# Query projections of a graph attention pass: three chunks made first, the others beside the first nine edge groups

## The chip, the cores and the metric

The kernel runs on one core of a Trainium2 chip. The metric is the device time of one execution in microseconds (us); lower is better. Engines: TensorE (PE, its weight loads PEld), VectorE (DVE), ScalarE (ACT), GpSimd (POOL), and SyncE (SP), which issues transfers. Engines run their own instruction streams and wait for each other through semaphores.

## The reference

A graph attention layer over 6250 nodes and 200,000 edges (sorted by destination), and then a mixture of eight experts over the nodes. What matters here is the attention:

```python
enh = node_features + 0.1 * query_emb            # node_features = layernorm(x), 6250 x 256
Q, K, V = enh @ Wq + bq, enh @ Wk + bk, enh @ Wv + bv      # 4 heads of 64
mod_k = K[src] + 0.2 * rel_w[edge_type][:, None, :]
scores = einsum('ehd,ehd->eh', Q[dst], mod_k) / 8          # softmax over the edges of a dst
agg = segment_sum(softmax_weight * V[src], dst)
x = x + layernorm(agg @ Wo + bo + node_features)
```

## The kernel before

The program has three stages, one after the other: `prepare`, `edge_pass` and `finish`, with a barrier of all engines (L645) between the first two. (`any_order_pass` stands under a condition on `unfit` and runs only for edges of an unusual order.)

**prepare.** 49 tiles of 128 nodes: layer norm, transposes into `QT` (features down the partitions, 2 x 6250 columns), K and V projections on TensorE, rows of K and V stored to DRAM (`kv`, 2 KB a node). Beside it VectorE works through a generator `setup()`, a step at a time between its tile operations: it makes each edge group's first node (`bases`), tests whether the edges are in the order that the pass needs (`unfit`), and casts the lists of source nodes, turned by TensorE into `psR`, into `idxall` (L914).

**edge_pass.** First `QT` is projected in place to the queries: 13 chunks `QCH` of 512 columns (the last 106). TensorE multiplies a chunk by `wq` into psD or psK in turn (L446, signal `s_q`), ScalarE adds the bias and copies it back over `QT` (L266, signal `s_qe`); TensorE may be two chunks ahead. Ahead of that, ScalarE copies the source lists of the first six groups from `idxall` into `idx` (`listed`, L256, signal `s_idx`), for which GpSimd's gathers wait.

Then 261 groups. A group is 384 edges of each of two streams (the lower and the upper half of the edges). Its 768 rows of K and V are gathered by six indirect DMAs of 128 rows that GpSimd issues (L246) into a ring of U = 6 slots; the gathers of group g + 6 wait for the sum of group g (`s_agg`). The engines are interleaved by `step(T)`: in the step of group g, TensorE turns the keys of g + 1 (`k_turned`, psK, L461), makes the scores of g (psD, L477 to L485), sums group g - 1 (psA, L496), hands on carried maxima and relation terms (psX, L525 and L527) and turns the weights of g (psP, L534). VectorE's `k_half` (L368) and ScalarE's (L291) copy the turned keys out; VectorE takes the maximum of psD (L393), ScalarE the exponentials (L311), the carried sums (`e_carried`, L302, which waits for the sum of a group) and the turned weights (L323). ScalarE also copies the 16-node windows of `QT` that group g + 1 needs, at offsets `bases`, into `qb` (L285). Steps from -1 to 7 are written out (`LO`, `WARM`), the rest is a loop of six steps a turn, with a short tail.

Groups 0 to 8 read only the start of each stream's range of nodes.

## Time and profile before

| | |
|---|---|
| median of 3 runs | 3803.58 us (3799.91 to 3803.76) |
| profiled execution, its own time | 3804.72 us |
| its span (first to last instruction) | 3802.4 us |
| TensorE busy | 3098.0 us, 81% |
| VectorE, ScalarE, GpSimd busy | 1690.1, 1507.6, 1962.7 us |
| mean granted TensorE clock | 0.870 of full |

Times in the rows are us from the start of the span. "Idle before <- X" tells how long the engine stood still ahead of an instruction and whose signal ended it; "remote" is a signal whose sender the profile doesn't name, "issue" is time with no wait that it shows. A matmul's start is recorded and its end is modelled.

### The profile page before, as it was taken

What the parts mean: (1) busy time and instruction counts of PE and PEld (TensorE: products, weight loads), DVE (VectorE), ACT (ScalarE), POOL (GpSimd) and SP (SyncE); (2) the same over time, 40 slices, a digit from 0 to 9 for tenths busy, and PEclk for the clock granted to TensorE, in tenths of its full rate; (3) what the DMA queues carried; (4) which work ended last, traced back from release to release, by engine and by line L of the source; (5) the groups of instructions that cost most, each with busy time, mean ns of one, the idle gap of its engine ahead of it and who ended that gap; (6) DMA issues with size and microseconds to landing.
All of it is one profiled execution on the core that took longest, in us unless ns stands there. A gap on an engine that the chain in (4) does not pass through costs nothing. (4 is left out here: it accounts for less than half of the span.)

```text
span 3802.4 us, 76627 instructions
## 1 busy us (share of the span) xinstructions
PE 3098.0 (81%) x21156; PEld 2146.9 (56%) x21156; DVE 1690.1 (44%) x6041; ACT 1507.6 (40%) x4739; POOL 1962.7 (52%) x2036
## 2 busy tenths in 40 slices
PE   8777787778777777877777777787667998899898
PEld 6444444444444444444444444444347898888798
DVE  6154444444444444444444444444475554553222
ACT  5333333333333333333333333333336565564232
POOL 6345555555555555655555555555345444432222
PEclk9888888888888888888888888888758999999999
DMA  6556766676666666666667666666475666665664
GB/s 221 164 150 187 191 190 184 186 191 189 185 185 191 189 185 188 187 192 185 189 187 190 188 185 187 190 188 185 138 230 151 203 203 184 194 180 156 194 181 131
DMA packets 292073, 700.68 MB, mean 184 GB/s; under 512 B 44040, under 2 KB 139679, under 8 KB 291796
## 3 DMA queue, kind: packets, MB, share of 16 engines
q0 software_dynamic: 151888, 455.79, 43.4%
q1 hardware_dynamic: 140036, 243.15, 21.0%
q8 instruction: 64, 1.05, 0.1%
q14 instruction: 85, 0.70, 0.1%
HBM read 632.80 MB, written 65.96 MB: 184 GB/s over the span
## 5 line engine op out<-in xcount | busy, mean ns | idle before, releaser
L246 POOL DMA_INDIRECT e_kv<-d_kv,e_idx x1566 | 1496.1, 955 | 1132.3 <-PE psA L496 668.5
L496 PE MATMUL psA<-e_kv,e_probT 128*32 128x128 f32 x6264 | 529.2, 286 | 297.9 <-issue 292.3
L393 DVE TENSOR_REDUCE e_small<-psD 128x1 f32<-128x384 f32 x261 | 145.5, 558 | 1219.6 <-remote 1208.6
L461 PE MATMUL psK<-consts,e_kv 128*128 128x128 f32 x3132 | 606.6, 327 | 3.3 <-ACT QT L266 1.0
L302 ACT ACTIVATE e_carried<-psA,e_small 128x130 f32<-128x130 f32 x261 | 96.7, 370 | 1135.1 <-PE psA L496 1115.4
L496 PEld LDWEIGHTS psA<-e_kv,e_probT 128*32 128x32 f32 x6264 | 199.9, 108 | 532.8 <-issue 503.8
L461 PEld LDWEIGHTS psK<-consts,e_kv 128*128 128x128 f32 x3132 | 427.5, 166 | 116.4 <-issue 110.0
L1975 PE MATMUL f_psY<-f_w,f_hT 128*128 x1680 | 396.6, 390 | 38.2 <-ACT f_hT L1570 22.1
L1500 POOL DMA_INDIRECT out<-f_y,f_whose x105 | 166.8, 1589 | 479.0 <-DMA out<-f_y,f_whose 281.7
L1962 PE MATMUL f_psH<-f_xT,f_w 128*128 128x128 f32 x3360 | 404.3, 280 | 0.4 <-issue 0.4
L1570 ACT ACTIVATE f_hT<-f_psH,f_b 128x128 f32<-128x128 f32 x840 | 237.6, 372 | 411.0 <-PE f_psH L1962 333.1
L1962 PEld LDWEIGHTS f_psH<-f_xT,f_w 128*128 128x128 f32 x3360 | 396.6, 196 | 3.0 <-issue 0.8
L1975 PEld LDWEIGHTS f_psY<-f_w,f_hT 128*128 128x128 f32 x1680 | 317.7, 195 | 86.2 <-issue 45.8
L285 ACT COPY e_qb<-QT 64x32 f32 x1044 | 229.3, 220 | 298.6 <-issue 279.5
L368 DVE COPY e_kT<-psK 128x384 f32<-128x384 f32 x522 | 286.7, 549 | 94.3 <-PE psK L461 84.0
L485 PE MATMUL psD<-e_kT,e_qb 128*32 128x384 f32 x2088 | 293.5, 644 | 0.0
L291 ACT COPY e_kT<-psK 128x384 f32<-128x384 f32 x522 | 247.0, 473 | 30.6 <-issue 23.9
L525 PE MATMUL psX<-e_small,e_carry 128*128 128x1 f32 x522 | 107.8, 271 | 174.2 <-DVE e_small L399 150.7
L525 PEld LDWEIGHTS psX<-e_small,e_carry 128*128 128x128 f32 x522 | 87.1, 207 | 246.4 <-issue 244.0
L534 PE MATMUL psP<-consts,e_prob 128*128 128x128 f32 x783 | 180.8, 352 | 49.5 <-ACT e_prob L311 42.0
L507 PEld LDWEIGHTS psA<-e_accs,e_carry 128*128 128x128 f32 x522 | 90.3, 218 | 227.2 <-issue 227.2
L1821 DVE TENSOR_SCALAR f_xT<-f_psT,f_ln 128x128 f32<-128x128 f32 x210 | 76.5, 406 | 307.8 <-PE f_psT L1952 218.9
(281 smaller groups left out, 4330.2 us busy)
## 6 DMA issues: line engine op xcount, KB each, us to landing
f_w<-in_W SPq DMA_DIRECT2D x113, 1024.0 KB
e_rows<-d_feat SPq DMA_DIRECT2D x174, 288.0 KB
e_kv<-d_kv,e_idx POOLq DMA_INDIRECT x1566
d_accs<-e_accs SPq DMA_DIRECT2D x87, 195.0 KB
f_xs<-d_xs SPq DMA_DIRECT2D x105, 129.0 KB
d_kv<-p_kv SPq DMA_DIRECT2D x48, 256.0 KB, 2.1
p_x<-in_x SPq DMA_DIRECT2D x49, 128.0 KB, 2.6
n_v<-d_kv SPq DMA_DIRECT2D x49, 128.0 KB
```

What stands on the lines that cost most here:

```text
L246: pool.indirect_dma_start(out=kv[g.slot][:, t, :], out_offset=None, in_=kv_dram[:, :], in_offset=bass.IndirectOffsetOnAxis(ap=idx[g.slot][ ...
L285: act.copy(qb[a.slot % R][o * HD:(o + 1) * HD, :].rearrange("p (c b w o) -> p c b w o", c=2, b=DC, o=2)[:, c, :, :, o], QT[o * HD:(o + 1) ...
L291: act.copy(kT[a.slot % 2][:, 1, j * GH:(j + 1) * GH], psK[:, 1, 0:GH]).then_inc(s_kTa, 1)
L368: dve.tensor_copy(kT[a.slot % 2][:, 0, j * GH:(j + 1) * GH], psK[:, 0, 0:GH]).then_inc(s_kTv, 1)
L461: mm = pe.transpose(psK[:, half, t * P:(t + 1) * P], kv[a.slot][:, third * TS + t, half * P:(half + 1) * P], ident)
L485: mm = pe.matmul(psD[own, g.slot % 2, 0:GH], qb[g.slot % R][:, own], kT[g.slot % 2][:, b, c * GH:(c + 1) * GH], start=False, stop=True, ti ...
L496: mm = pe.matmul(psA[own, 0:2 * HD], probT[c.slot % R][:, j, own], kv[c.slot][:, s * TS + j, D + b * P:D + (b + 1) * P], start=j == 0, sto ...
L525: pe.matmul(psX[:, 0:1], carry[a.slot][:, :], small[(a.slot - 1) % U][:, MM], start=True, stop=True)
L534: mm = pe.transpose(psP[:, j * P:(j + 1) * P], prob[g.slot % R][:, j * P:(j + 1) * P], ident)
L1570: act.activation(hT[:, f, :], psH[:, f // FB % 2, f % FB * BK:(f % FB + 1) * BK], ACT.Gelu, bias=b1[:, bass.ds(e * FC + f, 1)]).then_inc(s ...
L1962: mm = pe.matmul(psH[:, f // FB % 2, f % FB * BK:(f % FB + 1) * BK], w1[g % RW][:, a, f * P:(f + 1) * P], xT[g % 2][:, a, :], start=a == 0 ...
L1975: mm = pe.matmul(psY[:, 0:D], hT[:, f, :], w2[:, bass.ds(e * (FC * D) + f * D, D)], start=f == 0, stop=f == FC - 1)
```

## The change

Three query chunks, `EARLY = (0, 5, 6)`, are made ahead of the groups; the two streams' first nine groups read within them. The other ten are cut into 19 units of up to 256 columns (`LATER`), given to the steps -1 to 7 as 1, 3, 3, 2, 2, 2, 2, 2, 2 (`beside`). A unit is `ask(u)` on TensorE, into a PSUM bank of its own, `psL`, and `asked(u)` on ScalarE, which adds the bias and copies it over `QT`. From the second unit on, TensorE waits for the copy of the unit before. The first unit of a step with several stands behind the scores on TensorE and behind the exponentials on ScalarE; the others stand at the step's end. ScalarE waits at the end of such a step until its own copies are written, and ahead of the step's units until its window copies are.

The test `unfit` gets three more conditions, in `setup()`: that group 8's windows end within the chunks made first, and that the second stream doesn't begin ahead of chunk 5. If one fails, the fallback pass runs.

The six first row lists are copied by VectorE in `prepare`, at the end of `setup()`, and the buffers `idx` are allocated outside of both stages. GpSimd waits for `s_idx` from group 6 on only.

```diff
--- before.py
+++ after.py
@@ -137,7 +137,15 @@
 CONSTS, CAT = lay_constants()
 
 
-def edge_pass(nc, ctx, cst, QT, kv_dram, idxall, feat_dram, accs_dram, bases, delta, penc, relT, reach, keys, spots, wq, bqc):
+RING = 6
+EARLY = (0, 5, 6)
+QC = 512
+QH = QC // 2
+SURE = 8
+LATER = [(q, min(q + QH, N)) for c in range(-(-N // QC)) if c not in EARLY for q in range(c * QC, min(c * QC + QC, N), QH)]
+
+
+def edge_pass(nc, ctx, cst, idx, QT, kv_dram, idxall, feat_dram, accs_dram, bases, delta, penc, relT, reach, keys, spots, wq, bqc):
 
 
     def sb(name, shape, dt=F32):
@@ -146,9 +154,8 @@
     def sem(name):
         return ctx.enter_context(nc.semaphore(name))
 
-    U = 6
+    U = RING
     R = 3
-    idx = [sb(f"e_idx{i}", [P, TG], I32) for i in range(U)]
     rows = [sb(f"e_rows{i}", [P, HB, 2, GH], BF16) for i in range(U // HB)]
     kv = [sb(f"e_kv{i}", [P, TG, 2 * D]) for i in range(U)]
     relhot = [sb(f"e_relhot{i}", [P, GH], F32R) for i in range(R)]
@@ -172,6 +179,7 @@
     psP = ctx.enter_context(nc.psum_tensor("psP", [P, 512], F32))
     psA = ctx.enter_context(nc.psum_tensor("psA", [P, 512], F32))
     psX = ctx.enter_context(nc.psum_tensor("psX", [P, 512], F32))
+    psL = ctx.enter_context(nc.psum_tensor("psL", [P, DC, QH], F32))
     MX, MC, MM, NM, AL, SUM = (slice(i, i + 1) for i in range(6))
     CARRIED = slice(256, 256 + 2 * CW)
 
@@ -201,10 +209,13 @@
     s_px = sem("es_px")
     s_q = sem("es_q")
     s_qe = sem("es_qe")
-    QCH = [slice(q, min(q + 512, N)) for q in range(0, N, 512)]
+    QCH = [slice(c * QC, min(c * QC + QC, N)) for c in EARLY]
     psQ = (psD, psK)
 
     LO, HI, WARM = -1, 2, 8
+    share = [1, 3, 3] + [2] * (WARM - LO - 3)
+    beside = {LO + i: list(range(sum(share[:i]), sum(share[:i + 1]))) for i in range(WARM - LO)}
+    assert WARM <= SURE and sum(share) == len(LATER)
     AHEAD = U - 1
     SOON = NT - (NG + LO - WARM) // U
     assert 0 <= SOON < WARM
@@ -241,7 +252,7 @@
 
                     if g.first >= U:
                         pool.wait_ge(s_agg, g.t - (U - 1))
-                    hold(pool, s_idx, g.t + 1)
+                        hold(pool, s_idx, g.t - (U - 1))
                     for t in range(TG):
                         pool.indirect_dma_start(
                             out=kv[g.slot][:, t, :], out_offset=None, in_=kv_dram[:, :],
@@ -257,9 +268,6 @@
                          idxall[:, 0:2 * NG * TS].rearrange("p (c q) -> p c q", c=2)[:, :, bass.ds(t * TS, TS)]
                          ).then_inc(s_idx, 1)
 
-            for t in range(U):
-                listed(t, t)
-
             for i, q in enumerate(QCH):
                 act.wait_ge(s_q, i + 1)
                 for b in range(DC):
@@ -267,6 +275,13 @@
                                    bias=bqc[:, b:b + 1]).then_inc(s_qe, 1)
             act.wait_ge(s_qe, DC * len(QCH))
             act.wait_ge(s_init, 4)
+
+            def asked(u):
+                lo, hi = LATER[u]
+                act.wait_ge(s_q, len(QCH) + u + 1)
+                for b in range(DC):
+                    act.activation(QT[:, b, lo:hi], psL[:, b, 0:hi - lo], ACT.Identity, bias=bqc[:, b:b + 1]
+                                   ).then_inc(s_qe, 1)
 
             def step(T):
                 n = T(-AHEAD)
@@ -313,6 +328,11 @@
                                    accum_out=small[g.slot][:, SUM]).then_inc(s_exp, 1)
                     act.activation(small[g.slot][:, AL], small[g.slot][:, MC], ACT.Exp,
                                    bias=small[g.slot][:, NM], scale=SCALE).then_inc(s_exp, 1)
+                units = beside.get(g.t, []) if isinstance(g.t, int) else []
+                if units and a.live:
+                    act.wait_ge(s_qb, a.t * 4 + 4)
+                for u in units[0:-1][0:1]:
+                    asked(u)
                 if a.live:
                     k_half(a, 1)
                 if g.live:
@@ -321,6 +341,10 @@
                         act.wait_ge(s_agg, g.t - (R - 1))
                     act.wait_ge(s_pp, g.t + 1)
                     act.copy(probT[g.slot % R][:, :, :].rearrange("p t q -> p (t q)"), psP[:, 0:GH]).then_inc(s_pT, 1)
+                for u in units[len(units[0:-1][0:1]):]:
+                    asked(u)
+                if units:
+                    act.wait_ge(s_qe, DC * (len(QCH) + units[-1] + 1))
             pipeline(act, NG, -AHEAD, HI, U, WARM, step)
 
         @blk.vector
@@ -449,8 +473,19 @@
             pe.wait_ge(s_qe, DC * len(QCH))
             pe.wait_ge(s_init, 4)
 
+            def ask(u):
+                lo, hi = LATER[u]
+                if u >= 1:
+                    pe.wait_ge(s_qe, DC * (len(QCH) + u))
+                for b in range(DC):
+                    for a in range(DC):
+                        mm = pe.matmul(psL[:, b, 0:hi - lo], wq[:, a, b * P:(b + 1) * P], QT[:, a, lo:hi],
+                                       start=a == 0, stop=a == DC - 1)
+                mm.then_inc(s_q, 1)
+
             def step(T):
                 g, a = T(0), T(-1)
+                units = beside.get(g.t, []) if isinstance(g.t, int) else []
 
                 def k_turned(j):
 
@@ -486,6 +521,8 @@
                                            kT[g.slot % 2][:, b, c * GH:(c + 1) * GH],
                                            start=False, stop=True, tile_position=(0, own.start))
                     mm.then_inc(s_d, 1)
+                for u in units[0:-1][0:1]:
+                    ask(u)
                 c = T(1)
 
                 def summed(j):
@@ -533,6 +570,8 @@
                     for j in range(TS):
                         mm = pe.transpose(psP[:, j * P:(j + 1) * P], prob[g.slot % R][:, j * P:(j + 1) * P], ident)
                     mm.then_inc(s_pp, 1)
+                for u in units[len(units[0:-1][0:1]):]:
+                    ask(u)
             pipeline(pe, NG, LO, HI, U, WARM, step)
 
 
@@ -550,7 +589,7 @@
     return [(lo, bass.ds(node_rows(t) + lo, hi - lo), hi) for lo, hi in zip(cuts, cuts[1:])]
 
 
-def prepare(nc, ctx, cst, io, out, dram, QT, idxall, bases, delta, penc, relT, unfit, reach, keys, wq, wo, bqc, consts,
+def prepare(nc, ctx, cst, io, out, dram, idx, QT, idxall, bases, delta, penc, relT, unfit, reach, keys, wq, wo, bqc, consts,
             lnst, biaso):
 
 
@@ -593,6 +632,7 @@
     endsf = sb("p_endsf", [P, IT, P])
     misfit = sb("p_misfit", [P, 2 * len(chunks) + 2])
     misfits = sb("p_misfits", [P, 2])
+    early = sb("p_early", [1, 4])
     psT = [ctx.enter_context(nc.psum_tensor(f"p_psT{i}", [P, 512], F32)) for i in range(2)]
     psKV = [[ctx.enter_context(nc.psum_tensor(f"p_ps{n}{i}", [P, 512], F32)) for i in range(2)] for n in "KV"]
     psS = ctx.enter_context(nc.psum_tensor("p_psS", [P, 512], F32))
@@ -899,7 +939,15 @@
                     link(dve.tensor_copy(baseall[a * HW:(a + 1) * HW, :],
                                          reach[a * HW:(a + 1) * HW, a * NG:(a + 1) * NG]))
                 yield
-                link(dve.tensor_scalar(unfit[0:1, :], misfits[0:1, 1:2], 1.0, None, ALU.min))
+                link(dve.tensor_scalar(early[:, 0:1], basef[0:1, 0, SURE:SURE + 1], float(QC - W), None, ALU.is_gt))
+                link(dve.tensor_scalar(early[:, 1:2], basef[0:1, 1, 0:1], float(EARLY[1] * QC), None, ALU.is_lt))
+                yield
+                link(dve.tensor_scalar(early[:, 2:3], basef[0:1, 1, SURE:SURE + 1],
+                                       float((EARLY[2] + 1) * QC - W), None, ALU.is_gt))
+                link(dve.tensor_copy(early[:, 3:4], misfits[0:1, 1:2]))
+                yield
+                link(dve.tensor_reduce(misfits[0:1, 0:1], early[:, :], AX.X, ALU.add))
+                link(dve.tensor_scalar(unfit[0:1, :], misfits[0:1, 0:1], 1.0, None, ALU.min))
                 yield
                 link(dve.memset(delta[:, 0:1], 1000.0))
                 link(dve.tensor_tensor(delta[:, 1:NG], baseall[:, 1:NG], baseall[:, 0:NG - 1], ALU.subtract))
@@ -912,6 +960,12 @@
                         yield
                     dve.wait_ge(s_turn, i + 1)
                     dve.tensor_copy(idxall[:, c * P:(c + n) * P], psR[:, 0:n * P]).then_inc(s_back, 1)
+                    yield
+                dve.wait_ge(s_back, 1 + -(-IT // 4))
+                for t in range(RING):
+                    dve.tensor_copy(idx[t][:, :].rearrange("p (c j) -> p c j", c=2),
+                                    idxall[:, 0:2 * NG * TS].rearrange("p (c q) -> p c q", c=2)[:, :, t * TS:(t + 1) * TS]
+                                    ).then_inc(s_back, 1)
                     yield
 
             extra = setup()
@@ -2036,17 +2090,18 @@
             bases = sb1("bases", [1, 2, NG], I32)
             delta = sb1("delta", [P, NG])
             penc = sb1("penc", [P, NG])
+            idx = [sb1(f"idx{i}", [P, TG], I32) for i in range(RING)]
             relT = sb1("relT", [P, P])
             reach = sb1("reach", [P, 2 * NG])
             keys = sb1("keys", [P, 2 * NG])
             wq = sb1("wq", [P, DC, D])
             bqc = sb1("bqc", [P, DC])
             with ExitStack() as c1:
-                prepare(nc, c1, cst, io, out, dram, QT, idxall, bases, delta, penc, relT[:, :], unfit, reach, keys,
+                prepare(nc, c1, cst, io, out, dram, idx, QT, idxall, bases, delta, penc, relT[:, :], unfit, reach, keys,
                         wq, wo, bqc, consts, lnst, biaso)
             unfit_now = nc.values_load(unfit[0:1, 0:1], min_val=0, max_val=1)
             with ExitStack() as c2:
-                edge_pass(nc, c2, cst, QT, dram["kv"], idxall, dram["feat"],
+                edge_pass(nc, c2, cst, idx, QT, dram["kv"], idxall, dram["feat"],
                           dram["accs"][0:NG * P].rearrange("(g p) x -> g p x", p=P),
                           bases, delta, penc, relT[:, :], reach, keys, spots, wq, bqc)
```

## Rows read from the trace of the kernel before

**Rows 1.** The page: each engine's busy time, share and instructions

```profile
PE 3098.0 (81%) x21156; PEld 2146.9 (56%) x21156; DVE 1690.1 (44%) x6041; ACT 1507.6 (40%) x4739; POOL 1962.7 (52%) x2036
```

**Rows 2.** Windows: stretch, length, PE, PEld, DVE, ACT, POOL busy, clock, DMA share, GB/s

```profile
100.00:123.50 23.50, 22.57 (x114) 19.01 (x112) 10.50 (x46) 13.45 (x42) 0.00 (x0) 1.00 0.45 158
...
127.20:197.50 70.30, 48.80 (x105) 21.23 (x105) 1.37 (x13) 17.60 (x33) 34.27 (x36) 0.83 0.53 152
...
178.00:197.00 19.00, 17.87 (x40) 8.08 (x40) 0.00 (x0) 6.99 (x13) 0.00 (x0) 0.82 0.00 0
...
1000.00:1097.00 97.00, 76.51 (x547) 45.29 (x546) 41.75 (x152) 35.16 (x120) 56.44 (x60) 0.84 0.69 191
```

**Rows 3.** Timeline of TensorE, query stage: start, length, instruction, idle before

```profile
127.29 5.06 PE L446 MATMUL psD<-QT,wq 128*128 128x512 f32 x8 [3.84 <-PEq L645]
...
132.19 3.59 PE L446 MATMUL psK<-QT,wq 128*128 128x512 f32 x8
...
145.93 3.59 PE L446 MATMUL psK<-QT,wq 128*128 128x512 f32 x8
...
149.36 3.59 PE L446 MATMUL psD<-QT,wq 128*128 128x512 f32 x8
...
197.49 0.87 PE L461 MATMUL psK<-consts,e_kv 128*128 128x128 f32 x6 [0.96 <-ACT QT L266]
```

**Rows 4.** Timeline of ScalarE, query stage

```profile
128.43 0.69 ACT L256 COPY e_idx<-idxall 128x6 int32<-128x6 int32 x6
...
146.13 1.27 ACT L266 ACTIVATE QT<-psD,bqc 128x512 f32<-128x512 f32 x2 [2.17 <-issue]
...
156.34 1.27 ACT L266 ACTIVATE QT<-psK,bqc 128x512 f32<-128x512 f32 x2 [8.95 <-remote]
...
177.33 1.27 ACT L266 ACTIVATE QT<-psD,bqc 128x512 f32<-128x512 f32 x2 [19.72 <-remote]
```

**Rows 5.** Timeline of GpSimd: first, 36th, a late and last gather

```profile
129.51 1.07 POOL L246 DMA_INDIRECT e_kv<-d_kv,e_idx  x1 [55.46 <-ACT e_idx L256]
...
173.49 0.94 POOL L246 DMA_INDIRECT e_kv<-d_kv,e_idx  x1 [0.30 <-issue]
...
294.93 0.95 POOL L246 DMA_INDIRECT e_kv<-d_kv,e_idx  x1 [0.30 <-issue]
...
2701.55 0.95 POOL L246 DMA_INDIRECT e_kv<-d_kv,e_idx  x1 [0.30 <-issue]
```

**Rows 6.** Timelines of TensorE and VectorE: psD and the reduce that waits

```profile
202.86 0.85 PE L485 MATMUL psD<-e_kT,e_qb 128*32 128x384 f32 x8
...
224.05 1.51 PE L485 MATMUL psD<-e_kT,e_qb 128*32 128x384 f32 x8
...
226.35 0.56 DVE L393 TENSOR_REDUCE e_small<-psD 128x1 f32<-128x384 f32 x1 [1.31 <-PE psD L485]
...
290.96 0.85 PE L485 MATMUL psD<-e_kT,e_qb 128*32 128x384 f32 x8
...
297.10 0.56 DVE L393 TENSOR_REDUCE e_small<-psD 128x1 f32<-128x384 f32 x1 [5.57 <-remote]
...
2715.66 0.85 PE L485 MATMUL psD<-e_kT,e_qb 128*32 128x384 f32 x8
...
2716.58 0.56 DVE L393 TENSOR_REDUCE e_small<-psD 128x1 f32<-128x384 f32 x1 [0.36 <-PE psD L485]
```

**Rows 7.** Timeline of ScalarE: e_carried after a group's sum

```profile
210.54 0.37 ACT L302 ACTIVATE e_carried<-psA,e_small 128x130 f32<-128x130 f32 x1 [1.85 <-PE psA L496]
...
278.03 0.37 ACT L302 ACTIVATE e_carried<-psA,e_small 128x130 f32<-128x130 f32 x1 [4.26 <-PE psA L496]
...
2712.63 0.37 ACT L302 ACTIVATE e_carried<-psA,e_small 128x130 f32<-128x130 f32 x1 [3.90 <-PE psA L496]
...
2719.08 0.37 ACT L302 ACTIVATE e_carried<-psA,e_small 128x130 f32<-128x130 f32 x1 [2.14 <-PE psA L496]
```

**Rows 8.** Timeline of VectorE, first stage: the first cast of row lists

```profile
86.88 0.68 DVE L914 CAST idxall<-p_psR 128x512 int32<-128x512 f32 x1
```

## The prediction

> **What bounds the kernel now.** I read the page first [rows 1]: TensorE is busy 81% of the span, no other engine over 52%. The chain that ended last tells of the final stage alone, and the change ends long before it, so I read by stretches instead [rows 2]. Three stretches matter: the end of the first stage (100 to 123.5), the query stage from 127.2 to 197.5, and the loop over edge groups, of which 1000 to 1097 is a sample: TensorE is busy 76.51 of 97.00 there, at a granted clock of 0.84.
>
> The query stage is not what it looks like. Its 13 chunks start every 3.43 us where nothing stops them (132.19 to 149.36 is five of them) [rows 3], 45 us in all at most, yet the stage takes 70. The rest is two holes. TensorE's sixth and seventh chunk are recorded as done at 149.52 and 152.95, but ScalarE, which waits for nothing else, copies them out at 156.34 and 177.33 [rows 4]. The signal of TensorE comes late by 6.8 and 24.4 us. What goes on meanwhile: GpSimd issues its first 36 gathers without a pause, 129.51 to 174.44 [rows 5]; ScalarE's long wait ends 2.9 us after the last of them. From 178 on the DMA engines carry nothing [rows 2], and the chunks pass on at once.
>
> The same is seen in the edge groups. Around 290, psD's last matmuls are recorded to 291.81 and VectorE's reduce, which waits for them, starts at 297.10 [rows 6]; the last gather of that step ends at 295.88 on GpSimd [rows 5]. After the last gather of all (2701.55 [rows 5]) the same pair is 2716.51 and 2716.58. ScalarE's e_carried, one a group, comes every 9.64 us (210.54 to 278.03, seven steps) while gathers run, and 6.45 us apart (2712.63, 2719.08) when none is left [rows 7]. So the pass runs on a loop: a group's sum frees a ring slot, GpSimd issues six gathers (44.9 us for the first 36, so 7.5 for six [rows 5]), and the next sum comes some 2 us after the sixth. TensorE's idle time is 20.49 us of 97.00 [rows 2], some 2 us a step, and more when its clock is up.
>
> **The change, part by part.**
>
> Row lists. Six ScalarE copies (0.69 us together, 128.43 on) and the wait for them leave; GpSimd's first gather went out at 129.51 [rows 5] and can now go at about 127.3, when all engines enter the pass: 2.2 us sooner for all of the first 36. VectorE gets six copies of this kind (0.12 us each on ScalarE [rows 4]; at most 0.68, the wider cast of the row lists on VectorE itself [rows 8]) behind the casts of the row lists, the first of them at 86.88 and the last about 12 us later. Its busy time from 100 to 123.5 is 10.50 us of 23.50, TensorE's 22.57 [rows 2], so they lie beside TensorE's work: cost 0, bound 6 x 0.68 = 4 us if that cover were gone. The test adds five operations on one to four numbers in the same place: 0, bound 5 x 0.68 = 3 us, since none can take longer than that wide cast. Whether it can fire is plain from sizes: nine groups are 3,456 edges of 200,000 sorted ones over 6250 nodes, some 110 nodes; the nearest limit lies some 450 nodes above a stream's start (stream 1 starts near node 3120, its limit is 3568). So the fallback isn't taken.
>
> Ten chunks leave the query stage. TensorE does three chunks, from 127.29 to 132.19 + 3.43 + 3.59 = 139.2, and ScalarE's copies of one take 1.27: 140.5 [rows 3, 4]. The first transposes of edge rows stood at 197.49 and can stand at 140.9: 56.6 us sooner. That is 31 us of matmuls moved and 26 us of holes.
>
> What comes back, first part: to the first sum. Before, from 197.49 to the first e_carried at 210.54 it is 13.05 us, with no gather in flight [rows 3, 7]. The step before group 0 now holds one unit, group 0's step three, and group 1's step one ahead of the sum: five units of 256 columns, each half of 3.43, 1.72 us. Unhindered, that is 140.9 + 13.05 + 8.6 = 162.5, 48.0 us sooner than 210.54. Rows don't bind it: 7.5 us a group from 127.3, and at most some 3 us to land, gives group 1 at 145.2, and its step starts at 146. But these steps now run while the 36 gathers go out, and that is where the holes were. If the signal of psD of group 0 is held until 2.9 us after the last gather, 172.2 + 2.9 = 175.1, then the 6.8 us that lay between psD's end at 203.71 [rows 6] and 210.54 and three units (5.2) follow: 187.1, 23.4 us sooner. Those are the two ends. Signals passed freely until 146.13 in the query stage, and once in mid-burst (156.34) [rows 4], so neither end is natural; I take the middle, 35.7 us sooner.
>
> Second part: the other 14 units, two a step in seven steps, 24 us of matmuls (the last is short; I don't count that). TensorE without gathers needs 6.45 us a step [rows 7]; with two units 9.89, against 9.64 now. Lowest cost: 0.25 a step, 1.7 in all (a step can't get shorter than now, for the burst and what follows it stay: 7.5 + 2 us). Highest: all of it, 24. The step is held by the gathers' burst and not by TensorE's columns, psD being done up to 5.3 us before its signal [rows 6], so I take a value near the low end: 1 us a step, 7 us. ScalarE's part (half the 1.27 us of a chunk for each unit [rows 4]) fits the 61.8 us that it has free of 97.00 [rows 2]; the copies stand ahead of k_half and probT, whose readers are psK's next transposes and the sum, both behind the held signals. Its own wait at the step's end delays the next window copies by under 2.5 us; these are needed late in TensorE's step. SyncE's queue is not touched; its transfers of edge features go out at the pass's start, as now.
>
> Beyond step 7 nothing is changed: the same loop a group, the finish as before. The start of the pass is carried through to the end, since the ring then stands as it stands now.
>
> Sum: -35.7 + 7 = -28.7. The profiled execution took 3804.72 us (span 3802.4), so 3776.0; the median shown is 1.1 below it: 3775.
>
> The Trainium skill, page "SBUF — State Buffer", section "Who interferes with whom", says that DMA never contends with a compute engine, as its ports are its own. This case's trace doesn't show a slowed matmul, and yet signals 24 us late while gathers run, which that section has no word for. By its rule alone nothing would be held and the time would be that of the first rival.
>
> **Rivals.** (a) Nothing is held: the late signals belong to the query stage's own pattern. For it: up to 146 all pass, and in an early step with gathers in flight psD's signal is only 0.8 us late (225.56 to 226.35 [rows 6]). Time: -48.0 + 4 = -44, 3760. (b) Held to the end of the burst, with work exposed as above: -23.4 + 7, 3787. For it: the 24.4 us at 152.95 and the step around 290. (c) The units' hand-back is what gets late. Each unit waits for ScalarE's copy of the one before, and ScalarE waits for TensorE's signal, the very kind that is late by 5.3 us; behind ScalarE's wait stand the window copies of the next group. If each of 14 units costs its 1.72 us and a late signal of 3.05, the middle between 0.8 and 5.3, that is 67 against 35.7: 3835, slower. It decides from 2.6 us a unit on. Against it: unit two is asked for early in the burst, when signals pass. (d) The gain is paid back exactly: 2 to 3.1 us a unit, no measurable change.
>
> **How the numbers follow.** Forecast 0.41, (a) 0.22, (b) 0.20, (d) 0.09, (c) 0.08. A measurement can tell about 0.2% (7.6 us) from no change. The forecast, (a) and nearly all of (b) are faster by more than that: 0.80; the rest of (b) and (d) within it: 0.12; slower 0.08. The range goes from (a), 3758, to what (b) gives with 3 us exposed a step, near 3800. The likeliest case alone is 3766 to 3787.
>
> **What would show it.** The first gather near 127.3; the third copy of the query stage at 140.5; the first psK transposes at 141; e_carried of group 0 near 175 (163 for (a), 187 for (b)); from there seven intervals near 10.6 us (9.9 at best; over 12 for (c) or (d)), then 9.7 as now. TensorE's granted clock over those steps above the present 0.84, since the units fill its idle time. I am wrong if the first sum comes later than 187, if the intervals exceed 12 us, or if the first stage ends later than 123.9.

## The result: 82595 us, 21.7 times the time before

The changed kernel took 82595.36 us (median, 82581.09 to 82604.75) against 3801.74 us, a ratio of 21.718 (21.692 to 21.744). Forecast were 3775 us and a range of 3758 to 3799. The page of the profile after says at once where the time is: first the busy line that answers to [rows 1], then TensorE's granted clock in 40 slices, then the costliest groups.

```profile
PE 8331.8 (10%) x27728; PEld 3760.8 (5%) x27728; DVE 12190.8 (15%) x35006; ACT 1841.8 (2%) x6351; POOL 15490.8 (19%) x13236
...
PEclk8655555555555555555555555555555555555557
...
L1244 PE MATMUL g_psB<-g_spread,consts 125*125 125x500 f32 x3200 | 3247.4, 1118 | 68525.2 <-DVE g_spread L1215 68525.2
L1182 POOL DMA_INDIRECT g_q<-d_q,g_ends x1600 | 1960.8, 1225 | 42162.6 <-SPq L1165 42162.6
...
L257 POOL DMA_INDIRECT e_kv<-d_kv,idx x1566 | 1497.1, 956 | 1108.3 <-PE psA L533 652.9
```

L1182 and L1244 stand in `any_order_pass`, the fallback. It ran: 1600 rounds of 125 edges, in which no round begins before the one ahead of it has stored its results. Its first round's gather of `g_q` starts at 3035 us and its last at 81406, so 49.0 us a round. For 42162.6 / 1600 = 26.4 us of each GpSimd stands still between a round's last store and the next round's first gather. Most of that is not the next round's edge columns but the store itself, for whose landing GpSimd waits (`written`). One round as a sample: the store leaves GpSimd at 3161.50, SyncE issues the next columns from 3184.12 on, and the gather follows at 3189.14. The means over all rounds are 21.2 us to the columns' issue and 5.0 from there to the gather.

```profile
3160.30 1.20 POOL L1189 DMA_INDIRECT d_agg<-g_new,g_ends  x1 [0.31 <-issue]
3189.14 1.23 POOL L1182 DMA_INDIRECT g_q<-d_q,g_ends  x1 [27.64 <-SPq L1165]
```

```profile
3184.12 0.28 SPq L1170 DMA_DIRECT2D g_ends<-in_src  x1
```

The L257 row of the page is the fast pass with its 1566 gathers; it ran too, ahead of the fallback. Its windows answer to [rows 2], and its `e_carried` to [rows 7]:

```profile
100.00:123.50 23.50, 22.62 (x114) 19.11 (x112) 10.88 (x51) 13.56 (x41) 0.00 (x0) 1.00 0.46 158
127.20:197.50 70.30, 42.42 (x174) 26.17 (x174) 14.79 (x55) 17.53 (x46) 37.07 (x39) 0.71 0.58 165
1000.00:1097.00 97.00, 76.05 (x558) 44.68 (x558) 43.00 (x154) 34.98 (x120) 56.52 (x61) 0.85 0.67 187
```

```profile
193.42 0.37 ACT L317 ACTIVATE e_carried<-psA,e_small 128x130 f32<-128x130 f32 x1 [2.70 <-PE psA L533]
...
2710.24 0.37 ACT L317 ACTIVATE e_carried<-psA,e_small 128x130 f32<-128x130 f32 x1 [1.04 <-PE psA L533]
```

The first sum is 17.1 us sooner than 210.54, the last 23.6 sooner than 2733.80. So the part that I had forecast is in there, though the first sum gained less than half of the 35.7 us forecast for it, and 78.8 ms came behind it. The test that decides it is five more operations on VectorE, the four shown taking 0.13 or 0.14 us each, beside TensorE's work:

```profile
84.04 0.13 DVE L942 TENSOR_SCALAR p_early<-p_basef 1x1 f32<-1x1 f32 x1
84.21 0.14 DVE L943 TENSOR_SCALAR p_early<-p_basef 1x1 f32<-1x1 f32 x1
...
85.11 0.13 DVE L945 TENSOR_SCALAR p_early<-p_basef 1x1 f32<-1x1 f32 x1
...
85.96 0.14 DVE L950 TENSOR_SCALAR unfit<-p_misfits 1x1 int32<-1x1 f32 x1
```

**Why the test says unfit.** Its limits are written with `QC`, and the diff sets `QC = 512` at the head of the file. But the test stands in `prepare`, and `prepare` has had a local of that name all along (L601 before, L641 after): `QC, Q01, BV, BQ = range(4)`, columns of a small table of vectors. There `QC` is 0. So the limits are 0 - 16 = -16, 5 x 0 = 0 and 7 x 0 - 16 = -16 in place of 496, 2560 and 3568: "group 8's first node above -16" is true for any input, and the fallback always runs. `edge_pass` has no such local, so its chunks are 512 wide.

**Two conditions of the chip.** The kernel before itself took 3802 to 3850 us at some times and 3136 to 3139 us at others; each experiment below is compared only with the kernel before run beside it, and "slower condition" is that of the profiles before and after.

### The profile page after: what moved, and what is told of

It reads as the page before. It is cut to its first block and busy times, and to the rows that moved or that the text cites. A ratio compares the mean times of both kernels' runs of the same rounds, so it can differ in the third digit from the quotient of the medians.

```text
span 82587.8 us, 218267 instructions
## 1 busy us (share of the span) xinstructions
PE 8331.8 (10%) x27728; PEld 3760.8 (5%) x27728; DVE 12190.8 (15%) x35006; ACT 1841.8 (2%) x6351; POOL 15490.8 (19%) x13236
## 5 line engine op out<-in xcount | busy, mean ns | idle before, releaser
L1244 PE MATMUL g_psB<-g_spread,consts 125*125 125x500 f32 x3200 | 3247.4, 1118 | 68525.2 <-DVE g_spread L1215 68525.2
L1182 POOL DMA_INDIRECT g_q<-d_q,g_ends x1600 | 1960.8, 1225 | 42162.6 <-SPq L1165 42162.6
L1189 POOL DMA_INDIRECT d_best<-g_best,g_ends x1600 | 1944.1, 1215 | 20620.2 <-DVE g_new L1234 20620.2
L1244 PEld LDWEIGHTS g_psB<-g_spread,consts 125*125 125x125 f32 x3200 | 790.6, 308 | 69701.1 <-DVE g_spread L1215 69701.1
L1247 PE MATMUL g_psS<-g_weighted,g_same 125*125 125x260 f32 x3200 | 1967.4, 717 | 4658.8 <-DVE g_weighted L1228 4658.8
L1182 POOL DMA_INDIRECT g_kv<-d_kv,g_ends x1600 | 1939.6, 1212 | 487.6 <-issue 487.6
L1182 POOL DMA_INDIRECT g_old<-d_agg,g_ends x1600 | 1922.2, 1201 | 487.9 <-issue 487.9
L1189 POOL DMA_INDIRECT d_agg<-g_new,g_ends x1600 | 1920.3, 1200 | 487.6 <-issue 487.6
L1182 POOL DMA_INDIRECT g_best<-d_best,g_ends x1600 | 1920.0, 1200 | 487.9 <-issue 487.9
L1182 POOL DMA_INDIRECT g_rel<-in_rel,g_ends x1600 | 1919.8, 1200 | 488.3 <-issue 488.3
L257 POOL DMA_INDIRECT e_kv<-d_kv,idx x1566 | 1497.1, 956 | 1108.3 <-PE psA L533 652.9
```

The lines of the kernel that those rows point to most:

```text
L257: pool.indirect_dma_start(out=kv[g.slot][:, t, :], out_offset=None, in_=kv_dram[:, :], in_offset=bass.IndirectOffsetOnAxis(ap=idx[g.slot][ ...
L1182: pool.indirect_dma_start(out=out, out_offset=None, in_=table, in_offset=bass.IndirectOffsetOnAxis(ap=ends[0:GE, j:j + 1], axis=0)).then_i ...
L1189: pool.indirect_dma_start(out=table, out_offset=bass.IndirectOffsetOnAxis(ap=ends[0:GE, 1:2], axis=0), in_=rows_, in_offset=None).then_inc ...
L1244: pe.matmul(psB[0:GE, 0:H * GE], cst("ones")[0:GE, 0:GE], spread[0:GE].rearrange("p h e -> p (h e)"), start=True, stop=True).then_inc(summ ...
L1247: pe.matmul(psS[0:GE, 0:H * CW], same[0:GE, :], weighted[0:GE, :], start=True, stop=True).then_inc(summed, 1)
```

## The experiments

### The cause: the names alone, the test alone

`e1_renamed` and `e6_renamed_again` are the whole change with one local renamed, first in the faster condition, then in the slower (places apart in the file are parted by "..."):

```diff
-    QC, Q01, BV, BQ = range(4)
+    QE, Q01, BV, BQ = range(4)
...
-                sp.dma_start(cols[:, QC, :], down("query")).then_inc(s_kb, 16)
+                sp.dma_start(cols[:, QE, :], down("query")).then_inc(s_kb, 16)
...
-                link(dve.tensor_scalar(cols[:, Q01, :], cols[:, QC, :], 0.1, None, ALU.mult))
+                link(dve.tensor_scalar(cols[:, Q01, :], cols[:, QE, :], 0.1, None, ALU.mult))
```

> The whole change, with the column index in the first stage's function renamed from QC to QE, so that the test's limits are made from 512 again (496, 2560, 3568) and not from 0 (-16, 0, -16). Theory of the name collision: the test comes out 0, the slow pass over edges in any order isn't run, and what is left is the kernel that the prediction spoke of: 3775 us (e_carried of group 0 near 175, then seven intervals near 10.6), or 3760 where no signal is held (e_carried of group 0 near 163), 3787 where signals are held to the end of the burst (187), 3835 where the units' hand-back is late (intervals above 12). Rival: the test comes out 1 for another reason (the bases hold other values than I worked out from the input, or the reduce reads its operands too early): then the time stays near 82600 us.

> The change with the right limits once more, to see whether another chip shows what the first profile showed. On a chip like that of the first experiments: 0.9985 of before again. On a chip like that of the first profile the forecast would be tested as it stands: e_carried of group 0 near 175 and 28 us less (ratio 0.992), or 163 and 44 less (0.988) where no signal is late, 187 and 16 less (0.996) where they are held to the burst's end.

Measured: 3135.11 us against 3139.4, ratio 0.9985 (0.9976 to 0.9993), and in the slower condition 3785.03 against 3805.28, ratio 0.9945 (0.9933 to 0.9957). The fallback ran in neither. A name is the whole of the 78.8 ms.

`e2_test_alone`, `e12_test_alone_again` and `e17_test_alone_third` are one kernel: the kernel before with the constants and the seven lines of the test as the change writes them, nothing else. `e16_changed_again` is the changed kernel.

```diff
-                link(dve.tensor_scalar(unfit[0:1, :], misfits[0:1, 1:2], 1.0, None, ALU.min))
+                link(dve.tensor_scalar(early[:, 0:1], basef[0:1, 0, SURE:SURE + 1], float(QC - W), None, ALU.is_gt))
...
+                link(dve.tensor_scalar(unfit[0:1, :], misfits[0:1, 0:1], 1.0, None, ALU.min))
```

> The kernel before, with the test alone added as the change writes it (same names, limits from the shadowed QC). If the test alone takes the kernel into the pass over edges in any order, the time is the changed kernel's within some 50 us: 82590 to 82650 us. If the slow pass is entered for something else in the change (a misfit count spoilt by the new copies or by the queries made late), it is 3804 us, as before plus nothing.

> The kernel before with the test alone, again, under the condition of the profiles of before and after: if the first run's 77229 us differed from the changed kernel's 82595 for the chip's condition alone, it is 82600 to 82640 now (the changed kernel's, plus the some 35 us of query stage that it keeps); if the rest of the change matters beside the test, it stays some thousands of us below.

> The changed kernel as it stands. If the test accounts for all of it, its time is that of the kernel before with the test alone in the same condition, less the few us that the moved chunks gain: 77000 to 77300 us in the faster condition (the test alone took 77229 and 77050), 82580 to 82610 in the slower. If something else of the change costs beside the test, it lies hundreds of us above the test alone.

> The kernel before with the test alone, beside the changed kernel in one condition: within some 200 us of it in either (77050 and 77229 are what it took in the faster condition; 82595 is the changed kernel in the slower).

Measured, one execution each: 77229 and 77050 us in the faster condition; side by side in the slower one 79706 us for the changed kernel and 79700 for the test alone. The first forecast, 82590 to 82650, was missed by 5.4 ms, and so was the one for the changed kernel in the slower condition, 82580 to 82610, by 2.9 ms; the 82600 to 82640 for the slower condition was not put to the test, since that run fell into the faster one. The fallback's rounds vary from one time to another: 49.0 us each in the profile after, 47.2 in the changed kernel run again, 46.1 and 46.0 in the faster condition. Nearly all of it lies between a round's last store and the issue of the next columns, 21.2, 19.4 and (the first of the faster two) 18.3 us. That is more than the rest of the change is worth, but side by side the two kernels agree to 6 us. Nothing of the change but the test is needed for the fallback and its cost.

### The parts, in the faster condition

`e3_chunks_alone` has ScalarE copy the first row lists again. `e4_lists_alone` is the kernel before with only that part changed: `idx` laid by VectorE, and GpSimd's wait as in the change.

> The change with the right limits, but ScalarE copies the first row lists again at the start of the pass, as before: query chunks moved, and the test, alone. By the forecast the first gather goes out at 129.5 and not 127.3, and the whole is 0 to 2.2 us slower than the renamed kernel: if the first sum waits for gathers (forecast and the rival with signals held to the burst's end), 2.2 us slower; if nothing is held (first sum bound by the query stage and the chunks), the same within 1 us.

> The kernel before with one part of the change: VectorE lays the first six row lists in the first stage. The first gather goes out at 127.3 in place of 129.5, and the last of the first 36 at 172.2. If the query stage is held to the end of the burst, as I read it (ScalarE's long wait ended 2.9 us after the last gather), the query stage ends about 2.2 us sooner and the time is 2 us less; if its holes belong to the stage's own pattern, nothing changes (within 1 us).

Measured: 3135.15 us, 0.9984 (0.9975 to 0.9992), as the renamed kernel; and 3140.23 us, 0.9999 (0.9990 to 1.0008). The lists alone do nothing here. What the chunks do is seen on GpSimd: in the renamed kernel it is busy 73.54 us from 1000 to 1097 with 78 gathers, and with the 0.30 us behind each of them that is all of the time. First rows of the lists alone: GpSimd waits 14.28 us for the first sum ahead of its 37th gather. Then the renamed kernel: no wait there, but in each of five steps with two units.

```profile
187.86 0.95 POOL L245 DMA_INDIRECT e_kv<-d_kv,idx  x1 [14.28 <-PE psA L492]
```

```profile
175.11 0.94 POOL L257 DMA_INDIRECT e_kv<-d_kv,idx  x1 [0.30 <-issue]
...
199.97 0.94 POOL L257 DMA_INDIRECT e_kv<-d_kv,idx  x1 [2.66 <-PE psA L533]
210.10 0.94 POOL L257 DMA_INDIRECT e_kv<-d_kv,idx  x1 [2.94 <-PE psA L533]
...
238.63 0.94 POOL L257 DMA_INDIRECT e_kv<-d_kv,idx  x1 [1.06 <-PE psA L533]
```

The wait before the 37th gather is gone, 14.0 us, and 2.36 + 3 x 2.64 + 0.76 = 11.0 are paid back (each wait less the 0.30 that stands there anyway; the other two of 2.94 stand in the place of the last "..."). The 3.0 left are near the 4.3 between the medians of the renamed kernel and the kernel before. A step with two units takes 10.13 us here, and GpSimd needs 7.5 for its six gathers.

### One unit a step

`e7_one_a_step` is the renamed kernel with the nineteen units spread over nineteen steps; `e8_two_early` makes chunks 0 and 6 first and spreads 21 units. `e5_before` is the kernel before, for its trace, and `e19_one_a_step_again` is `e7_one_a_step` once more.

```diff
-SURE = 8
+SURE = 20
...
-    LO, HI, WARM = -1, 2, 8
-    share = [1, 3, 3] + [2] * (WARM - LO - 3)
+    LO, HI, WARM = -1, 2, 20
+    share = [1] * len(LATER) + [0] * (WARM - LO - len(LATER))
```

> The kernel before, unchanged, for its trace beside the others of the same chip. The renamed kernel ran 4 us under the kernel before (3135 against 3139), where the profile shown before the prediction had the whole at 3802 and a group every 9.8 us. If the chip of this batch is like that of the first experiments, the query stage has no holes here (thirteen chunks 3.43 us apart, as with VectorE's lists alone), GpSimd's 37th gather waits some 14 us for the first sum (172.6 to 187), and groups come 7.55 us apart on average, as fast as GpSimd issues. If it is like the chip of the first profile, holes of some 26 us in the query stage and 9.8 us a group, 3802 in all.

> The change with the right limits, but one unit beside each of the first nineteen steps instead of one, three, three and two; the steps written out are 21 and the test looks at group 20. Theory, GpSimd's issue bounds the pass: with two units a step takes 10.13 us against the 7.5 in which GpSimd issues six gathers, so GpSimd waits for slots and 11 us of the 14 us gained at the 37th gather are paid back; with one unit a step takes some 8.2 us, 0.7 above GpSimd's, which the slack of the first sum (some 10 us) covers, so GpSimd never waits and the whole is some 11 us less than the renamed kernel, 14 less than before: ratio 0.9955 on a chip like the first experiments'. Rival, the first sum's time carries through as in my forecast: then spreading the units changes only the first steps, the same 24 us of matmuls are paid, and the ratio stays within 1 us of the renamed kernel's 0.9985.

> As the kernel with one unit a step, with two chunks made first (0 and 6) instead of three, and 21 units. The query stage is 3.4 us shorter and the first sum comes that much sooner, but two more steps carry a unit. If GpSimd's issue bounds the pass and never waits in the kernel before this one, there is nothing left to gain: the same within 1 us. If it still waits there, this one is up to 3 us faster.

> The change with the right limits and one unit a step, again, beside it. Under the slower condition 0.991 of before as the last time. Under the faster one, where GpSimd's issue bounds the pass, 11 us under the renamed kernel's 0.9985: 0.9955, since GpSimd no longer waits for a slot.

All fell into the slower condition: the kernel before 3799.97 us; one unit a step 3771.06 against 3805.28, 0.9909 (0.9894 to 0.9924), and 3821.2 against 3850.07 on another chip, 0.9915 (0.9902 to 0.9928); two early 3775.4, 0.9924 (0.9911 to 0.9937), not told apart from it. So one unit a step is 14 us under the renamed kernel by the medians; in the profiled executions its eighth sum is 9.9 us sooner and its last 7.4, so some of the 14 lies behind the pass, where nothing was changed. My reason for it, GpSimd waiting for slots in the faster condition, was not what it met: no run shows this kernel in that condition. What it met: `e_carried` comes at 191.69 and then every 9.74 us from the first step on, as in the loop (259.83 for the eighth, 269.75 in the renamed kernel). A second unit is what lengthens a step.

### Where the first sum is held

Rows of the renamed kernel in the slower condition: TensorE, then VectorE, GpSimd and ScalarE.

```profile
145.28 1.89 PE L482 MATMUL psL<-QT,wq 128*128 128x256 f32 x8
...
162.01 1.51 PE L520 MATMUL psD<-e_kT,e_qb 128*32 128x384 f32 x8
178.29 3.78 PE L482 MATMUL psL<-QT,wq 128*128 128x256 f32 x8 [14.77 <-ACT QT L283]
...
191.00 1.99 PE L482 MATMUL psL<-QT,wq 128*128 128x256 f32 x8
```

```profile
159.90 0.47 DVE L440 CAST e_qrel_high<-psX 64x64 fp32r<-64x64 f32 x2 [14.84 <-remote]
...
179.35 0.55 DVE L417 TENSOR_REDUCE e_small<-psD 128x1 f32<-128x384 f32 x1
```

```profile
171.54 0.94 POOL L257 DMA_INDIRECT e_kv<-d_kv,idx  x1 [0.30 <-issue]
196.06 0.94 POOL L257 DMA_INDIRECT e_kv<-d_kv,idx  x1 [23.57 <-PE psA L533]
```

```profile
177.40 0.84 ACT L283 ACTIVATE QT<-psL,bqc 128x256 f32<-128x256 f32 x2 [25.36 <-remote]
...
195.37 0.37 ACT L317 ACTIVATE e_carried<-psA,e_small 128x130 f32<-128x130 f32 x1 [2.71 <-PE psA L533]
```

The first unit is done at 147.17 and ScalarE copies it at 177.40, 30 us late and 4.9 after the 36th gather ends (172.48). TensorE's next unit waits for that copy, so four more units and group 1's part of the step all come after 177.40, 18.0 us in all. In the faster condition, where no signal was held, the same kernel takes 16.6 us for the same stretch:

```profile
149.34 0.84 ACT L283 ACTIVATE QT<-psL,bqc 128x256 f32<-128x256 f32 x2 [1.64 <-PE psL L482]
...
165.96 0.37 ACT L317 ACTIVATE e_carried<-psA,e_small 128x130 f32<-128x130 f32 x1 [2.72 <-PE psA L533]
```

The other 1.4 us are the clock's, as far as the rows tell (no run takes it apart): with TensorE nearly idle from 163 to 178 its granted clock was 0.50 of full, and it stayed there to 184; the unit at 178.29 took 3.78 us, a later one 1.99. With one unit a step, only one unit stands behind the held copy (177.55) and not four, and yet the first sum came at 191.69, 3.7 us sooner than here. So three units of the four are worth 3.7 us, and most of the 18 is the step's own work behind a held signal.

`e13_gathers_after` and `e15_gathers_after_again` take the gathers away from the query stage, in both conditions:

```diff
+            pool.wait_ge(s_qe, DC * len(QCH))
             pipeline(pool, NG, 0, 0, U, WARM, step)
```

> The kernel before, but GpSimd's first gather waits until the query stage is done. Theory, TensorE's signals are held while gathers are issued: the thirteen chunks come 3.43 us apart with no hole and the query stage ends near 175, the first gather goes out there, the burst of 36 ends near 219.5, and now the first group's signals are held: e_carried of group 0 near 229, 18 us later than before, ratio 1.0048. Rival, the holes are the query stage's own: it ends at 197.5 again, the first gather goes out there and all is later by the rows' arrival, e_carried near 222. Rival, gathers hold nothing behind a first stage: e_carried near 197, 14 us less, ratio 0.9963. In the condition without late signals GpSimd's issue is the bound and starts 46 us later: some 30 us more, ratio 1.01.

> The kernel before with GpSimd's first gather held back until the query stage is done, once more. Under the slower condition: if the gathers in flight make TensorE's signals late, the thirteen chunks come 3.43 us apart and end near 175, the burst ends near 219.5, e_carried of group 0 near 229, ratio 1.0048; if the holes are the query stage's own, it ends at 197.5 and e_carried comes near 222 with the burst still behind it (242 if held to its end). Under the faster condition 34 us more, ratio 1.011, as the last time.

Measured: 3824.35 us against 3802.28, 1.0055 (1.0042 to 1.0069), in the slower condition, with `e_carried` of group 0 at 230.15 (229 by the theory that gathers hold the signals, 222 and 197 by its rivals); 3169.94 against 3135.8, 1.0111 (1.0096 to 1.0127), in the faster. ScalarE's copies in the slower one, the 13 chunks without a hole; then GpSimd, TensorE and VectorE behind them:

```profile
131.79 1.27 ACT L267 ACTIVATE QT<-psD,bqc 128x512 f32<-128x512 f32 x2 [3.33 <-PE psD L447]
...
148.95 1.27 ACT L267 ACTIVATE QT<-psK,bqc 128x512 f32<-128x512 f32 x2 [2.17 <-PE psK L447]
...
170.71 0.59 ACT L267 ACTIVATE QT<-psD,bqc 128x106 f32<-128x106 f32 x2
```

```profile
172.20 1.07 POOL L246 DMA_INDIRECT e_kv<-d_kv,e_idx  x1 [98.83 <-ACT QT L267]
...
216.10 0.95 POOL L246 DMA_INDIRECT e_kv<-d_kv,e_idx  x1 [0.30 <-issue]
```

```profile
192.30 1.51 PE L486 MATMUL psD<-e_kT,e_qb 128*32 128x384 f32 x8
```

```profile
218.69 0.56 DVE L394 TENSOR_REDUCE e_small<-psD 128x1 f32<-128x384 f32 x1 [26.55 <-remote]
```

The holes moved with the gathers: none in the query stage, and psD's signal 24.9 us late (193.81 to 218.69), passing 1.6 us after the last of the 36. What no run separates is whether GpSimd's issuing of the gathers or their traffic on the DMA engines holds the signals.

`e18_ring_of_four` shortens the burst itself, on the kernel with one unit a step (`DEEP = 4`; the first copy counts two more on `s_idx`, so that both waits still have one count):

```diff
                     if g.first >= U:
-                        pool.wait_ge(s_agg, g.t - (U - 1))
-                        hold(pool, s_idx, g.t - (U - 1))
+                        pool.wait_ge(s_agg, g.t - (DEEP - 1))
+                        hold(pool, s_idx, g.t - (DEEP - 1))
+                    elif g.first >= DEEP:
+                        hold(pool, s_agg, g.t - (DEEP - 1))
...
-                         ).then_inc(s_idx, 1)
+                         ).then_inc(s_idx, 1 + U - DEEP if isinstance(t, int) and t == U else 1)
```

> The kernel with one unit a step, but GpSimd runs four groups ahead of the sums and not six: the first burst has 24 gathers. Under the slower condition (before at 3802): if the first sum is held to the end of the first burst, which is 15 us shorter now, e_carried of group 0 comes at 177 in place of 191.7, and nothing after it changes, since each later burst of six follows a sum there: ratio 0.987 of before, 15 us under the kernel with one unit a step. If the delay belongs to the units or to the clock, e_carried stays near 191 and so does the time (0.991). Under the faster condition GpSimd's issue bounds the pass and runs 11.6 us behind a sum with six groups of slack; with four it waits for the sums: slower than with six, by more than 1%.

Measured: 3841.86 us against 3850.07, 0.9977 (0.9968 to 0.9986), where 0.987 was expected, and 21 us above the kernel with six slots beside it. The first sum is at 175.34, where the kernel beside it with six slots had 189.78, as expected of the burst. "Nothing after it changes" was wrong: the last `e_carried` is at 2754.96 against 2737.27, so a step takes (2754.96 - 175.34) / 260 = 9.92 us and not 9.80, and 32 us are lost where 14 were won. TensorE's granted clock is 0.80 from 1000 to 1097, against 0.84 beside it; which of the two follows from the other isn't shown. Why a shorter ring slows the loop stays open.

### The loop, 0.05 us a group

In the slower condition the renamed kernel's loop is shorter than before, which I had not forecast. `e9_lists_alone_again` is the lists alone once more. `e11_one_wait` and `e14_one_wait_again` move nothing; they only put ScalarE's first six list copies on a semaphore of their own, so that GpSimd waits for one count on both semaphores in the loop (GpSimd's side of the edit; on ScalarE's, those six copies signal `s_first`):

```diff
-                    hold(pool, s_idx, g.t + 1)
+                        hold(pool, s_idx, g.t - (U - 1))
+                    else:
+                        hold(pool, s_first, g.t + 1)
```

> VectorE lays the first six row lists, GpSimd's loop waits for the same count on both semaphores, nothing else of the change; this time under the condition of the profile before (3800 us). Theory A: GpSimd's two waits at the head of each group (the sum's and the row list's) have one count now and are one instruction (43 ns in the renamed kernel's trace) where they were two (start to start 76 ns, 50 ns more in all), and in a loop in which GpSimd is released by the sum and the sum by the burst's end every one of 255 groups is 50 ns shorter: 12.7 us, and 2.2 more for the earlier first gathers: ratio 0.9961, period 9.735 in place of 9.785. Theory B: the shorter period of the renamed kernel comes from the query chunks or their memory: then 2.2 us at most, ratio 0.9994, period 9.785.

> The kernel before, with nothing moved: ScalarE still copies the first six row lists at the start, but on a semaphore of their own, so that in the loop GpSimd waits for the same count on the sum's and on the row lists' semaphore. Theory A (two wait instructions become one): 12.7 us less, ratio 0.9967, the time from e_carried to GpSimd's next gather 0.683 in place of 0.733. Theory B (memory or VectorE's part matters): no change. In the condition in which groups come 7.55 us apart GpSimd isn't released by the sum, and neither theory gives a change.

> The kernel before with GpSimd's two waits of a group merged into one, nothing else, once more. Under the slower condition (before at 3802): if the merged wait is what shortened the renamed kernel's loop, 12.7 us less, ratio 0.9967, and 0.683 us from e_carried to the next gather in place of 0.733, period 9.735; if not, no change. Under the faster condition no change (0.9997 the last time).

Measured: in the faster condition 0.9996 (0.9987 to 1.0005) and 0.9997 (0.9988 to 1.0006), no change; in the slower one 3787.81 us against 3802.28, 0.9966 (0.9953 to 0.9979), against 0.9967 expected. `e_carried` to GpSimd's next gather is 0.73 us before (median of groups 20 to 219) and 0.68 with the merged wait, as expected. The lists alone have not been run in the slower condition. GpSimd's waits between 400 and 2600 us in that condition, of the kernel before, of the merged wait alone, and of the renamed kernel (total us, times, longest):

```profile
POOL e_kv L246 <- PE psA L496: 573.0, 225, 2.9
```

```profile
POOL e_kv L249 <- PE psA L499: 558.2, 226, 2.9
```

```profile
POOL e_kv L257 <- PE psA L533: 555.2, 224, 2.9
```

These are 2.55 us a wait before, 2.47 and 2.48 after. The release of GpSimd lies on the path from one sum to the next, and one instruction less there is worth 14 us over 261 groups.

## Why the prediction was wrong, point by point

**The step that failed** is this one: "Whether [the test] can fire is plain from sizes ... the nearest limit lies some 450 nodes above a stream's start ... So the fallback isn't taken." The sizes were right: with 512 the test doesn't fire, and the time is 3785 us. With the 0 that the name holds in `prepare` it fires for any input, and the time was 82595. I read the value of `QC` from the line of the diff that sets it and didn't look up what the name stands for in the function where the test is. No rival had the fallback at all, though the diff touches `unfit`, the one number that switches a pass of 1600 serial rounds on. A chance for that, with its price beside it, was owed: even at 1 in 100 the price is 788 us.

The other steps can be read in the renamed kernel, slower condition, beside the kernel before run with it:

| step | forecast | measured |
|---|---|---|
| first gather | 127.3 | 127.63 |
| third copy of the query stage starts | ends the stage at 140.5 | 140.45 (ends 141.7) |
| `e_carried` of group 0 | 175, between 163 and 187 | 195.37 (before: 211.23) |
| sooner by | 35.7, lowest 23.4 | 15.9 |
| seven intervals | 10.6 | 10.63 (before: 9.64) |
| 14 units | 7 us | 6.9 us |
| clock over these steps | above 0.84 | 0.95 (210 to 280) |
| the loop after | as now | 12.9 us less to the last sum |
| whole | -28.7 us | -20.3 us (0.9945) |

**The query stage** was right: ten chunks gone, the first transposes at 141.8 where 140.9 was forecast. **The late signals** were read rightly as the gathers' doing, and shown to be so in the slower condition (gathers after the query stage, ring of four).

**The first sum** was mis-sized, and came past the 187 that I had set as my own bound. The bound took the release 2.9 us after the last gather and 12.0 us of work behind it; the release came after 4.9, and 18.0 us of work stood behind it. The held signal was not only psD's but that of the first unit, which stands ahead of it on ScalarE, and from there the work is 16.6 us even where nothing is held; 1.4 us more fit the half clock. So the 8.3 us past the bound are 2.3 for the release, 4.6 of work that I hadn't counted behind it, and 1.4 most likely for the clock. That the second unit waited for the first one's held copy is a piece of rival (c), in the first burst alone; its price a unit, 3.05 us more for a late signal, was not paid later: of the five intervals with two units four took 10.13 to 10.31 us in the slower condition and the fifth 10.75, against 10.13 in the faster. Of the cases forecast, (b) came nearest to the first sum.

**The 14 units** were right in sum, 7 against 6.9, but not for my reason. I took a value near the low end because the gathers' burst holds a step; these steps took nearly what they take where nothing is held, so the units set their length, and half of the 6.9 is the one interval with three units (13.06 us).

**The row lists** were right in place (first gather at 127.63); whether the 2.2 us counted for them was gained, no run of them alone shows in the slower condition. I had missed that they also merge a wait, and the loop was 12.9 us shorter: "GpSimd waits for `s_idx` from group 6 on only" was in the diff, and I costed the wait that left, not the wait that stayed.

These two errors, 19.8 too good and 12.9 too bad, cancel all but 6.9 us, so the renamed kernel, 0.9945 x 3801.74 = 3781 us, would lie within the range; that it is near 3775 is in good part luck.

**Rival (a)**, nothing held, is what the faster condition showed: the renamed kernel's first sum came at 165.96, near its 163, though GpSimd's pace left only 4 us of it. The Trainium skill, page "SBUF — State Buffer", section "Who interferes with whom", has DMA never contend with a compute engine; the traces of the faster condition agree (a unit copied within 0.1 us of its recorded end in mid-burst, 149.30 to 149.34), and in those of the slower one the matmuls aren't slowed either at full clock (a unit takes 1.89 to 2.00 us in both), but their signals come up to 30 us late while gathers are issued, which the section has no word for.

## What to carry to other kernels

When a change writes to the flag of a fallback, work out the flag with the values that the names have in that very function, and give the fallback's price a line among the rivals, however small its chance. A constant added at the head of a file is worth a search for its name in every function that uses it; here one line of `prepare` told it. And in a loop in which one engine is released by another, count the instructions between the wait and the first useful one: one less was worth 14 us here in the slower condition, nearly as much as the 15.9 that the moved chunks gained at the first sum, and nothing in the faster, where GpSimd isn't released by the sum.

## What the runs showed of the hardware

- The kernel before took 3805 us at one time and 3139 at another on the same chip, and the experiments' four chips each fell into one or the other condition for all the runs made side by side. In the faster one 13 query chunks run without a hole beside the same 36 gathers and a group takes 7.55 us, GpSimd's own pace; in the slower one TensorE's signals are late while gathers are issued (147.17 to 177.40, 193.81 to 218.69) and a group takes 9.8 us. From 400 to 2000 us VectorE's reduce starts 3.9 us (median) after psD's recorded end in the profile before, and 0.07 in the renamed kernel in the faster condition. What puts the chip in either is open.
- Two waits for one count were one instruction of 43 ns on GpSimd where two counts took two with 76 ns from start to start, 0.05 us of each group.
- An indirect gather of 125 rows in the fallback takes 1.20 to 1.23 us on GpSimd, one of 128 rows in the ring 0.95. A store through GpSimd that the next round waits for cost 18.3 to 21.2 us from its end on GpSimd to the next round's first issue.
